# Two streams in one megakernel: where the next attention's norm is made, who stacks the queries, and how the bit layer quantises

## The reference, cut to what matters

```
for a in 0..3:
    x = x + tanh(g_xattn[a]) * attention_a(layernorm(x), ctx)
    x = x + tanh(g_ffn[a])   * experts_a(layernorm(x))
attention 0, 1, 2: 16 heads of 8 features, softmax over 256 keys
    (0: relu on q, k, v; 1: adjacency and a mask per batch are added to the scores, output
     projection; 2: one fixed mask, output projection)
attention 3: one head of 64, softmax, head tiled 16 times, output projection
experts 0: gate network and 8 experts 128 -> 512 -> 128 with selu, top 2
experts 1: two linear layers on activations quantised to 8 bit and weights of three values,
           exact gelu between ("bit layer"); the quantising scale of a row needs its norm and its maximum
experts 2: 8 experts with silu(h1) * h3 and low-rank parts, top 2
experts 3: 8 heads of 16 features, 16 experts with gelu, top 2
```

## Time and profile before

| | us |
|---|---|
| median of 3 runs | 1921.5 (1919.56 to 1936.71) |
| profiled execution | 1916.38 |
| its span | 1914.6 |
| mean granted clock of TensorE | 0.841 |

### The profile page before, as it was taken

How to read it: one execution, slowest core, us unless ns; L and a number is a source line. 1 busy time by engine, 2 the same in 40 slices (tenths; PEclk the granted TensorE clock), 3 DMA queues, 4 the chain that set the end, 5 groups by cost and what they waited for, 6 DMA issues and landing times.

```text
span 1914.6 us, 21114 instructions
## 1 busy us (share of the span) xinstructions
PE 1348.0 (70%) x7836; PEld 666.6 (35%) x7836; DVE 987.2 (52%) x2268; ACT 751.5 (39%) x1102; POOL 402.5 (21%) x462
## 2 busy tenths in 40 slices
PE   3456978865647697867477797886473869886756
PEld 2223544441212334531222455444121233453211
DVE  3347546656563453462552664666656445346252
ACT  0034643522324143337266463353232413433636
POOL 4306020025030200015332601001503020001424
PEclk9988999987559898969578898999755989896969
DMA  8204112112020200012420311300202020001221
GB/s 269 37 7 77 51 48 63 34 39 40 1 33 2 34 1 1 1 28 88 66 73 23 83 45 38 74 23 12 45 1 33 1 33 2 1 1 17 94 61 61
DMA packets 49221, 78.57 MB, mean 41 GB/s; under 512 B 15056, under 2 KB 34272, under 8 KB 48496
## 3 DMA queue, kind: packets, MB, share of 16 engines
q0 software_dynamic: 18752, 34.69, 7.7%
q1 hardware_dynamic: 25616, 25.25, 6.3%
q10 hardware_dynamic: 4752, 17.30, 2.9%
HBM read 52.63 MB, written 2.10 MB: 29 GB/s over the span
## 4 chain that ended last, share of the span: by engine, by line
PE 53%; DVE 18%; issue 12%; ACT 9%; DMA 4%; POOL 3%; SPq 1%; POOLq 0%; ACTq 0%; DVEq 0%
PE ps L705 5%; PE ps L587 5%; PE ps L721 5%; PE ps L538 5%; DVE nm L1205 4%; PE ps L809 4%; PE ps L863 3%; PE ps L543 3%; PE ps L811 3%; PE ps L852 3%; PE ps L799 3%; ACT hT L1075 3%; DVE ps L1221 2%; PE ps L570 2%; DVE hT L1403 1%
## 5 line engine op out<-in xcount | busy, mean ns | idle before, releaser
L341 POOL TENSOR_TENSOR rstd<-vare,mhalf 128x4 f32<-128x4 f32 x40 | 42.4, 1063 | 1191.2 <-DVE vare L1145 1131.2
L1205 DVE TENSOR_REDUCE nm<-ps 128x4 f32<-128x1024 f32 x192 | 231.8, 1222 | 113.9 <-PE ps L543 113.1
L965 ACT ACTIVATE pT<-ps 128x1024 f32<-128x1024 f32 x192 | 194.2, 1026 | 166.9 <-DVE ps L1221 103.8
L1075 ACT ACTIVATE hT<-ps,w_l_b 128x512 f32<-128x512 f32 x256 | 158.2, 684 | 91.6 <-PE ps L852 89.8
L705 PEld LDWEIGHTS ps<-l_ring,hT 128*128 128x128 f32 x1152 | 154.1, 206 | 79.7 <-issue 78.0
L705 PE MATMUL ps<-l_ring,hT 128*128 128x128 f32 x1152 | 157.8, 291 | 26.6 <-DVE acc L1343 25.1
L1403 DVE SCALAR_TENSOR_TENSOR hT<-ex,rl 128x512 f32<-128x512 f32 x144 | 104.4, 730 | 123.2 <-ACT rl L1014 99.2
L721 PE MATMUL ps<-xT,l_ring 128*128 128x512 f32 x288 | 164.9, 664 | 4.0 <-ACT rl L1014 4.0
L1013 ACT ACTIVATE ex<-ps,l_exp_bias 128x512 f32<-128x512 f32 x144 | 99.2, 689 | 172.3 <-PE ps L721 171.8
L852 PE MATMUL ps<-ex,w1s 96*128 96x512 bf16 x256 | 101.5, 438 | 75.2 <-ACT hT L1075 49.8
L587 PE MATMUL ps<-pT,vA 128*32 128x256 f32 x1536 | 122.8, 447 | 33.0 <-ACT oT L945 31.3
(11 more groups left out here) (256 smaller groups left out, 2097.7 us busy)
## 6 DMA issues: line engine op xcount, KB each, us to landing
l_ring<-in_l_wio ACTq DMA_DIRECT2D x33, 512.0 KB, 3.8
gate<-f_gate_rows POOLq DMA_DIRECT2D x64, 256.0 KB, 3.7
kS<-kp POOLq DMA_DIRECT2D x144, 64.0 KB, 3.5
qS<-qp SPq DMA_DIRECT2D x144, 64.0 KB
w_l_w<-in_l_w SPq DMA_DIRECT2D x3, 1024.0 KB
ex<-gate POOLq DMA_DIRECT2D x24, 128.0 KB, 5.3
pT<-in_l_wo SPq DMA_DIRECT2D x1, 2048.0 KB
m<-in_mask_q POOLq DMA_DIRECT2D x4, 512.0 KB, 6.2
```

The lines of the kernel that those rows point to most:

```text
L965: act.activation(pT[:, v % NPB, :], scores, ACT.Exp).then_inc(sem("p_ready"), 1)
L1075: act.activation(hid3[:, n % 8, :], bank(5 + n % 2), ACT.Gelu, bias=W["l3_b1"][:, ep:ep + 1])\
L1205: dve.tensor_reduce(nm[:, 2 * b:2 * b + 2, :, j].rearrange("p t g -> p g t"), ps[:, sl:sl + 2, :].rearrange("p g (t k) -> p g t k", t=2), ...
```

## The change: what it does

- After each expert layer of blocks 0 to 2, DVE, POOL, PE and ACT make layernorm, transposes and copy for the next attention of the same stream (`next_norm`, `next_T`; bank 6). Attention of blocks 1 to 3 starts without them; block 0 keeps its own. An expert layer starts on PE once that copy is out of bank 6 (`start_experts`).
- In attention, q is projected right after k and split before v is read out.
- The query stack: half 0 by six DMAs on SP, half 1 by six on POOL (`queries`), with a semaphore each.
- `FIRST_SLOT` is 18, and with it `END` 7 less.
- The query side of block 1's bias is made in the mask's own buffer (`m1f`), and all the bias work has other due times.
- `quantise` yields between its parts, the bit layer's due times are spread up to 54, its roots on POOL have due times 7 and 29.

```diff
@@ -70,7 @@
-FIRST_SLOT, SLOT = 25.0, 1.3
+FIRST_SLOT, SLOT = 18.0, 1.3
@@ -165,6 @@
+m1f = m1[:].rearrange("p t k -> p (t k)").bitcast(f32).rearrange("p (t k) -> p t k", t=NT)
@@ -349,19 @@
+        to = (m1f, bfull)[side]
-        step(pool.tensor_scalar(bfull[:], m1[:], 0.0, NEG, ALU.is_equal, ALU.mult))
+        step(pool.tensor_scalar(to[:], m1[:], 0.0, NEG, ALU.is_equal, ALU.mult))
-            step(pool.tensor_tensor(bfull[:, 2 * b:2 * b + 2, :], bfull[:, 2 * b:2 * b + 2, :],
+            step(pool.tensor_tensor(to[:, 2 * b:2 * b + 2, :], to[:, 2 * b:2 * b + 2, :],
-        step(pool.tensor_copy(b1q[:, 0], bfull[:]))
-        step(pool.tensor_tensor(bfull[:], bfull[:], b1q[:, 0], ALU.subtract))
-        step(pool.tensor_copy(b1q[:, 1], bfull[:]))
+        if i:
+            pool.wait_ge(*upto("s1", place(i - 1, 1), 2 * NK))
+        step(pool.tensor_copy(b1q[:, 0], m1f[:]))
+        step(pool.tensor_tensor(m1f[:], m1f[:], b1q[:, 0], ALU.subtract))
+        step(pool.tensor_copy(b1q[:, 1], m1f[:]))
@@ -379,36 @@
+    def queries(m):
+        pool.wait_ge(*upto("qp", m, 1))
+        for n, part in enumerate(X_PARTS):
+            row = 64 + DH * n
+            pool.dma_start(qS[row:row + DH, :, :], qp[64:128, part, :]).then_inc(sem("q_stack_1"), 16)
-        if a == 3:
-            root(i)
-        else:
+        if a < 3:
-            root(i)
+            if a == 0:
+                root(i)
+            yield 5.0 if a else 11.0
+            queries(place(i, a))
-                yield 10.0
+                yield 12.0
-                yield 14.0
+                yield 24.0
+                yield 34.0
+                query_bias(i - 1)
-                yield 24.0
-                query_bias(i - 1)
-                yield 32.0
+                yield 48.0
-                yield 10.0
+                yield 20.0
+                yield 34.0
+                bias(i + 1, 0)
+                yield END - 12.0
+                query_bias(i + 1)
+                mask_in(i + 1, 1)
-                yield 5.0
-                bias(i, 0)
-                mask_in(i, 1)
-                yield 12.0
-                query_bias(i)
-                yield 22.0
+                yield 16.0
@@ -422,10 @@
-        yield 0.0
-            root(i)
-            yield 16.0
+            for at in BIT_ROOTS:
+                yield at
+                root(i)
+        if n < 3:
+            yield OVER[n] + 1.0
@@ -492,11 @@
-    def norm_T(i, n):
+    def norm_T(i, n, to=2):
-            last = pe.transpose(bank(2)[:, t * P:(t + 1) * P], xn[i % 2][:, t, :], W["ident"][:])
+            last = pe.transpose(bank(to)[:, t * P:(t + 1) * P], xn[i % 2][:, t, :], W["ident"][:])
@@ -518,15 @@
+        if a == 0:
+            yield 6.0
+            norm_T(i, LN_OF_ATT[a])
+            yield 7.5
+        pe.wait_ge(*of("xT_ready", i, 7, n_T(LN_OF_ATT[a])))
+        pe.matmul(bank(3), W[L + "wq"][:], xT[s][:], start=True, stop=True).then_inc(sem("q_ps"), 1)
-        yield 6.0
-        norm_T(i, LN_OF_ATT[a])
-        yield 7.5
-        pe.wait_ge(*of("xT_ready", i, 7, n_T(LN_OF_ATT[a])))
-        pe.matmul(bank(3), W[L + "wq"][:], xT[s][:], start=True, stop=True).then_inc(sem("q_ps"), 1)
@@ -603,8 @@
-        for name in ("k_stack", "q_stack"):
-            pe.wait_ge(sem(name), 16 * HP * NSEG * (m + 1))
+        pe.wait_ge(sem("k_stack"), 16 * HP * NSEG * (m + 1))
+        for g in range(HP):
+            pe.wait_ge(sem(f"q_stack_{g}"), 16 * NSEG * (m + 1))
@@ -651,9 @@
-        yield 6.0
-        norm_T(i, LN_OF_ATT[3])
-        yield 7.5
@@ -689,6 @@
+    def start_experts(i, n):
+        experts_over(pe, (i, n))
+        last = before((i, n), 1)
+        if last is not None and last[1] < 3:
+            pe.wait_ge(*of("xT_ready", last[0], 7, n_T(LN_OF_ATT[last[1] + 1])))
+    def next_T(i, n):
+        norm_T(i, LN_OF_ATT[n + 1], 6)
@@ -707,7 @@
-        experts_over(pe, (i, 0))
+        start_experts(i, 0)
@@ -737,30 @@
+        yield OVER[0] + 3.0
+        next_T(i, 0)
-        experts_over(pe, (i, 1))
-        yield 6.0
+        start_experts(i, 1)
+        yield 16.0
-        yield 8.0
+        yield 18.0
-            yield 8.0 + t
+            yield 18.0 + t
-        yield 26.0
+        yield 44.0
-            yield 26.0 + t
+            yield 44.0 + t
@@ -768,18 @@
-            yield 31.0 + t
+            yield 49.0 + t
+        yield OVER[1] + 3.0
+        next_T(i, 1)
-        experts_over(pe, (i, 2))
+        start_experts(i, 2)
@@ -826,12 @@
+        yield OVER[2] + 3.0
+        next_T(i, 2)
-        experts_over(pe, (i, 3))
+        start_experts(i, 3)
@@ -901,10 @@
-    def norm_T(i, n):
+    def norm_T(i, n, at=2):
-        act.activation(xT[i % 2][:], bank(2), ACT.Copy).then_inc(sem(f"xT_ready_{i % 2}"), 1)
+        act.activation(xT[i % 2][:], bank(at), ACT.Copy).then_inc(sem(f"xT_ready_{i % 2}"), 1)
@@ -929,9 @@
-        yield 7.0
-        norm_T(i, LN_OF_ATT[a])
-        yield 8.5
+            yield 7.0
+            norm_T(i, LN_OF_ATT[a])
+            yield 8.5
@@ -978,9 @@
-        yield 7.0
-        norm_T(i, LN_OF_ATT[3])
-        yield 8.5
+        yield 3.0
@@ -1021,24 @@
+        yield OVER[0] + 4.0
+        norm_T(i, LN_OF_ATT[1], 6)
-        yield 7.0
+        yield 17.0
-        yield 12.0
-        for t in range(NT):
+        for t in range(NT):
+            yield 20.0 + 1.4 * t
-            yield 27.0 + t
+            yield 45.0 + t
+        yield OVER[1] + 4.0
+        norm_T(i, LN_OF_ATT[2], 6)
@@ -1056,6 @@
+        yield OVER[2] + 4.0
+        norm_T(i, LN_OF_ATT[3], 6)
@@ -1067,7 @@
-            yield (15.4 + 0.8 * n) if n < 8 else 31.0 + 3.0 * (n // 4 - 2) + 0.6 * (n % 4)
+            yield (15.8 + 0.8 * n) if n < 8 else 31.3 + 3.0 * (n // 4 - 2) + 0.6 * (n % 4)
@@ -1170,12 @@
-        src = x[s] if a else xn[s]
-        statistics(i, src)
-        yield 4.0
+            statistics(i, xn[s])
+            yield 4.0
+            dve.wait_ge(sem(f"x_copied_{s}"), i // 2 + 1)
+            normal(i, xn[s])
+            yield 10.0
+        else:
+            yield 3.0
+        dve.wait_ge(*upto("qf", m, 1))
+        step(dve.tensor_copy(qp[:, 0, :], qf[:]))
+        step(dve.tensor_tensor(rest_a, qf[:], qp[:, 0, :], ALU.subtract))
+        step(dve.tensor_copy(qp[:, 1, :], rest_a))
+        dve.tensor_tensor(qp[:, 2, :], rest_a, qp[:, 1, :], ALU.subtract).then_inc(sem("qp"), 1)
+        yield 10.5 if a == 0 else 5.0
@@ -1187,16 @@
-        yield 5.0
-        if a == 0:
-            dve.wait_ge(sem(f"x_copied_{s}"), i // 2 + 1)
-        normal(i, src)
-        yield 10.0
-        dve.wait_ge(*upto("qf", m, 1))
-        step(dve.tensor_copy(qp[:, 0, :], qf[:]))
-        step(dve.tensor_tensor(rest_a, qf[:], qp[:, 0, :], ALU.subtract))
-        step(dve.tensor_copy(qp[:, 1, :], rest_a))
-        dve.tensor_tensor(qp[:, 2, :], rest_a, qp[:, 1, :], ALU.subtract).then_inc(sem("qp"), 1)
@@ -1270,14 @@
-        yield 0.0
-        statistics(i, x[s])
-        yield 5.0
-        normal(i, x[s])
@@ -1344,11 @@
-    def quantise(i, src, dst, F, n):
+    def quantise(i, src, dst, F, n, at, gap, done):
+        yield at + gap
@@ -1356,12 @@
+        yield at + 2 * gap
+        yield at + 3 * gap
-        return dve.tensor_scalar(dst, src, -MAGIC, None, ALU.add)
+        yield at + 4 * gap
+        dve.tensor_scalar(dst, src, -MAGIC, None, ALU.add).then_inc(sem(done), 1)
+    def next_norm(i, n):
+        statistics(i, x[i % 2])
+        yield OVER[n] + 2.0
+        normal(i, x[i % 2])
@@ -1402,38 @@
-        yield SLOT_0 * (N0 + 8)
+        yield OVER[0]
+        yield from next_norm(i, 0)
-        yield 0.0
+        yield 6.0
-        quantise(i, xn[s][:], qx, D, 0).then_inc(sem("f1_qx"), 1)
-        for t in range(NT):
-            yield 10.0 + t
+        yield from quantise(i, xn[s][:], qx, D, 0, 6.0, 2.0, "f1_qx")
+        for t in range(NT):
+            yield 18.6 + t
-        yield 18.0
+        yield 28.0
-        quantise(i, hh[:], qh, F0, 1).then_inc(sem("f1_qh"), 1)
-        yield 36.0
+        yield from quantise(i, hh[:], qh, F0, 1, 28.0, 2.6, "f1_qh")
+        yield OVER[1]
+        yield from next_norm(i, 1)
@@ -1474,9 @@
-        yield SLOT_2 * (N2 + 2) + 4.0
+        yield OVER[2]
+        yield from next_norm(i, 2)
@@ -1584,10 @@
-            for g in range(HP):
-                row = 64 * g + DH * n
-                sp.dma_start(qS[row:row + DH, :, :], qp[64 * g:64 * g + 64, part, :])\
-                  .then_inc(sem("q_stack"), 16)
+            row = DH * n
+            sp.dma_start(qS[row:row + DH, :, :], qp[0:64, part, :]).then_inc(sem("q_stack_0"), 16)
@@ -1623,6 @@
+BIT_ROOTS = (7.0, 29.0)
+OVER = (SLOT_0 * (N0 + 8), 54.0, SLOT_2 * (N2 + 3) + 10.0)
```

## The result

| | before | after |
|---|---|---|
| median, us | 1926.5 (1919.6 to 1936.7, 4 runs) | 1985.1 (1978.4 to 1985.4, 4 runs) |
| ratio | | 1.029, 95% interval 1.023 to 1.035 |
| profiled execution: span | 1914.6 | 1983.6 |
| its mean granted clock | 0.841 | 0.822 |

The account below looks back on a forecast made before the run. PE was taken as nearly full beside selu from the first score on, but waiting ahead of it for the late query stack. Terms summed to −30.1 us on 1916.4: 1886.3 profiled, 1891 on the median's scale, stated 1889, range 1850 to 1932.

Parts of the forecast that it names:

- Step (c): Stall savings by step, with three fewer selu chunks ahead of the first score; selu after attention 0: −5.6 us.
- the last thing that would show the forecast wrong: Selu steps longer by more than the tail: PE lacks the three chunks it ran before the first score; no size.
- (a): Norm at the expert layer's end: 5.0 us exposed behind selu, 1.9 extra beside silu, nothing in the bit layer.
- (b): Split query stacks: landing 3.5 to 5 us instead of 8.4; first score about 22 us after k matmul, 25 beside selu.
- rival 2: Stack landing not shortened, only SP's issue time of about 4 us saved: 1914 us, chance 0.18.
- (d): Bit layer's quantising in pieces moves into the score stretch: +6.2 us beside attention 2, +8 beside attention 1.
- rival 3: Bit steps slower because DVE's quantising pieces lie uncovered on the path: +47.6 us, 1936 us, chance 0.15.
- Rival 1: PE's clock stays up in the bit step beside attention 1, some 8 us saved twice: 1873 us, chance 0.25.

Follow-up runs that it names:

- experiment 1: The changed kernel with FIRST_SLOT back at 25 and nothing else undone: 1905.6 us, ratio 0.989 to the kernel before.
- experiment 5: The changed kernel, FIRST_SLOT 18, with DVE's selu gate chain due 17.8 in place of 21.4, ahead of the first row maximum: 1968.5 us.
- experiment 14: The changed kernel, FIRST_SLOT 18, with the bit layer's due times behind its first pieces 7 earlier: 1978.2 us.
- experiment 3: The changed kernel with all twelve query DMAs on SP's queue again, POOL issuing only the keys: 2003.5 us against 1985.1.
- 8: The changed kernel with FIRST_SLOT 25 and half 1 of the query stack issued by ACT instead of POOL: 1912.0 us against 1905.6.

## Why the prediction was wrong, point by point

**FIRST_SLOT, the step that failed.** Step (c) let the three chunks shrink PE's work ahead of the first score, and booked the smaller idle as a gain ("idle 13.3 becomes 7.7, −5.6"; by its own figures, 26.5 less 18.6, it is 7.9). That is sound bookkeeping only if the first score moves up as far as forecast and if the chunks cost nothing more elsewhere. It moved from 38.2 to 31.1 instead of 26.5 and beside attention 1 not at all; what the chunks had filled was paid behind the attention (6.8 and 8.5, experiment 1); and the order behind it changed too: the gate's chain fell among the maxima (8 us beside attention 0, experiment 5), the chunks fell otherwise among the values (8 us beside attention 1, read from the traces) and the bit pieces behind the first slots (10.6 in the bit steps, experiment 14). Undone, the constant gives 79 us. With it undone the change measures −21, where the whole forecast was −30. I had named the mechanism as the last thing that would show the forecast wrong, and gave it no price and no place among the rivals.

**(a) Norm at the end.** The 5.0 behind a selu layer is right: the stretch behind the attention grew by 5.6 in both steps (19.5 to 25.1, 19.3 to 24.9, experiment 1), and putting it back gave 4.8. Missing was what the new PE order does to `kf`: I allowed a chunk and q's copy ahead, 1.2 more, and measured 1.7 to 2.7 more. Since POOL's eighteen issues hang on it, the early x^T gave no earlier first score beside attention 1 and cost 5.7 and 3.5. In all the early norm loses 42 behind selu and silu and gains 8.5 behind the bit layer, the place where I had it hidden.

**(b) The stacks, and rival 2.** The landing after POOL's last issue is 7.6 to 12.1 us, not 3.5 to 5; first scores came at 25.7 to 27.2 in the bit and silu steps where I had about 22 to 24.7, and 27.6 to 34.2 after the k matmul in selu steps for 25. The 8.4 that I halved was one of twelve such times in the trace of before, where they run from 3.9 to 11.3; that half the queue lands in half the time was never tested on them. Rival 2 had the mechanism, and of the 96 us missed it had priced 25. The page of after has the median from issue to landing (last figure, where it has one):

```profile
kS<-kp POOLq DMA_DIRECT2D x144, 64.0 KB, 3.8
...
qS<-qp POOLq DMA_DIRECT2D x72, 64.0 KB, 6.5
```

The Trainium skill (DMA: Bandwidth & Descriptors, "Issuing engines are not separate DMA queues") says that starting DMAs from several engines saves the sequencers' time alone, as they all run on the same sixteen. The runs agree that a second or third queue buys little: 18 us over twelve stacks (experiment 3), 0.7 to 2.1 us of a bit step's first score (8). They don't bear out that it is issue time alone: in experiment 3 the last issue came 1.4 us sooner and the first score 1.7 later.

**(d) Quantising in pieces, and rival 3.** The score parts of the bit steps grew by 7.8 and 8.1 (76.9 to 84.7, 63.1 to 71.2) where I had 8 and 6.2. Beside attention 1 that agreement was luck: with slot 25 it is 76.5, as long as before, and the slot made the 7.8. What the pieces cost there is not separated from the clock, which was 0.81 with slot 25 and 0.68 before. Beside attention 2 it is 69.5: +6.4, as forecast. Rival 3 did not occur.

**Rival 1.** The clock did not stay up: 0.70 in the score part beside attention 1 (0.68 before over the same cut), 0.86 beside attention 2 (0.91). With slot 25 these are 0.81 and 0.79: up in the one, as the rival had it, down in the other.

**The right parts.** First score earlier by 9 us in both bit steps and 6.8 in the silu step; bit and silu steps shorter; attention 3 longer, though by 8.2 for 3.4 in the first half.

## What to carry to other kernels

Work of the second stream that fills a wait is free only in that wait: before you let it shrink, check what ends the wait, since a filler taken from it is paid at the place where it goes. When a constant shifts the due times of one generator against all others, list every instruction of the others that changes sides, on each engine; here that was a gate chain on DVE, the pieces of the bit layer, the copy of k on ACT and, on POOL, a mask load that a wait had held back. A norm taken ahead paid here where it ended within a step that covered it, and lost where a step ended with it.
